# A new order of steps for three of five blocks, and scan decays by halves in two PSUM banks in one of them (state-space scan, attention and mixture-of-experts kernel)

## The reference

```python
x = x + scan_layer(group_norm(x))      # in_proj, 3x3 conv, silu, 4 scan paths, norm, gate, out_proj
t = tokens(x)
t = t + attention_causal(layer_norm(t))           # 12 heads of 16
u = layer_norm(t)
u = u + attention(ln1(u))                          # second attention, not causal
u = u + gelu(u @ mlp_w1 + b1) @ mlp_w2 + b2        # 192 -> 768 -> 192
xm = ln2(u)
u = u + sum_over_4_experts(top2_gate * (gelu(xm @ w1 + b1) @ w2 + b2))
out = t + u
```

## Time and profile before

| | us |
|---|---|
| median of 3 runs (lowest, highest) | 873.56 (868.95, 879.3) |
| the profiled execution, its own time | 875.49 |
| its span, first to last instruction | 873.8 |
| PE busy (share of the span) | 640.4 (73%) |
| DVE busy | 547.7 (63%) |
| ACT busy | 307.6 (35%) |
| POOL busy | 215.3 (25%) |
| mean granted TensorE clock | 0.846 of full speed |

### The profile page before, as it was taken

One profiled execution on the slowest core, in us unless ns is written; L12 is line 12 of the kernel. 1 busy time (PEld: TensorE's weight loads), 2 busy tenths in 40 slices (PEclk: granted clock), 3 DMA queues, 4 the chain that ended last, 5 costly groups with the idle time before them and its releaser, 6 DMA issues. The chain is left out here.

```text
span 873.8 us, 8707 instructions
## 1 busy us (share of the span) xinstructions
PE 640.4 (73%) x3156; PEld 429.7 (49%) x3156; DVE 547.7 (63%) x936; ACT 307.6 (35%) x576; POOL 215.3 (25%) x184
## 2 busy tenths in 40 slices
PE   2479556835677787858778778857787888896697
PEld 2233234423223574646346565645345657765596
DVE  4749656576998547765997556757995355442211
ACT  2324031234331132653543223563442424442131
POOL 4429511212343101031543101132452011001000
PEclk9989965757888678888899788878998899998789
DMA  6985000354670000373660003273630000000000
GB/s 143 299 170 151 0 9 1 47 145 113 161 172 25 9 1 10 48 201 93 161 152 10 9 0 38 71 191 93 175 92 9 1 1 1 1 1 10 0 1 10
DMA packets 26641, 61.69 MB, mean 71 GB/s; under 512 B 4928, under 2 KB 12752, under 8 KB 26608
## 3 DMA queue, kind: packets, MB, share of 16 engines
q1 hardware_dynamic: 26608, 61.26, 30.2%
HBM read 53.52 MB, written 3.54 MB: 65 GB/s over the span
## 5 line engine op out<-in xcount | busy, mean ns | idle before, releaser
L1895 POOL TENSOR_TENSOR state<-state,C_rows 128x1024 f32<-128x1024 f32 x42 | 113.1, 2692 | 178.4 <-DVE state L1445 156.8
L1445 DVE TENSOR_TENSOR_SCAN state<-decay,dx_rows 128x512 f32<-128x512 f32 x72 | 105.8, 1510 | 9.9 <-PE py L980 6.9
L980 PE MATMUL py<-state,sel 128*96 128x512 f32 x168 | 91.9, 681 | 14.8 <-POOL state L1895 14.6
L1765 ACT ACTIVATE decay<-d_rows,a_neg 128x255 f32<-128x255 f32 x144 | 61.1, 496 | 94.5 <-DMA d_rows<-delta_dram 58.8
L1052 PE MATMUL pd<-w_dn,act 128*128 128x192 f32 x480 | 90.5, 343 | 3.7 <-ACT act L1778 3.7
L1052 PEld LDWEIGHTS pd<-w_dn,act 128*128 128x128 f32 x480 | 82.7, 200 | 7.1 <-ACT act L1778 4.6
L1036 PE MATMUL pu<-fT,w_up 128*128 128x256 f32 x180 | 65.9, 452 | 12.4 <-ACT act L1778 11.9
L1438 DVE TENSOR_TENSOR dx_rows<-dx_rows,B_rows 128x1024 f32<-128x1024 f32 x36 | 58.4, 1621 | 12.5 <-DMA dx_rows<-delta_x_dram 12.5
L792 PE MATMUL ps<-hT,w_qkv 96*96 96x256 f32 x128 | 41.5, 495 | 33.4 <-DVE hT L1583 32.7
L1936 POOL TENSOR_TENSOR cT<-cT,inv_den 128x256 f32<-128x256 f32 x24 | 19.9, 831 | 174.3 <-DVE inv_den L1642 174.3
L1778 ACT ACTIVATE act<-pu,b_up 128x256 f32<-128x256 f32 x90 | 37.7, 470 | 71.3 <-PE pu L1040 71.1
(11 more groups left out here) (285 smaller groups left out, 1220.0 us busy)
## 6 DMA issues: line engine op xcount, KB each, us to landing
dx_rows<-delta_x_dram SPq DMA_DIRECT2D x41, 512.0 KB, 5.1
d_rows<-delta_dram SPq DMA_DIRECT2D x36, 512.0 KB, 6.6
d_rows<-delta_x_dram SPq DMA_DIRECT2D x6, 512.0 KB, 5.1
w_dn<-exp_w_dram SPq DMA_DIRECT2D x1, 2304.0 KB
B_rows<-xdbl SPq DMA_DIRECT2D x4, 512.0 KB, 7.0
C_rows<-xdbl SPq DMA_DIRECT2D x4, 512.0 KB, 10.7
w_up<-exp_w_dram SPq DMA_DIRECT2D x1, 1536.0 KB
delta_x_dram<-delta_x SPq DMA_DIRECT2D x4, 384.0 KB, 3.4
```

The source lines that it names most:

```text
L980: mm = nc.tensor.matmul(py[0:INNER, :], sel[:, first:first + INNER], flat(states[g % held])[:, paths], start=False, stop=(g == GROUPS - 1) ...
L1445: ins = nc.vector.tensor_tensor_scan(flat(states[g % held])[:, both], flat(decay[g % 2])[:, both], dx_rows[g % 2][:, both], 0.0, ALU.mult, ...
L1765: ins = nc.scalar.activation(decay[g % 2][:, k, rest], d_rows[g % 2][:, k, rest], ACT.Exp, scale=a_neg[:, at:at + 1])
L1895: nc.gpsimd.tensor_tensor(now, now, C_rows[:, :], ALU.mult).then_inc(sc_done, 1)
```

## The change

Two things change; the arithmetic does not.

1. **Plans.** `FIRST`, `STEADY` and `LAST` get new orders; `OPENING` and `CLOSING` keep theirs. Every step is still there. Steps move between slots, so only the order within each engine changes.
2. **Decays by halves.** With `one_decay = run_s and run_a and not run_f`, which holds in FIRST alone, `decays(g)` and `scan(g)` are replaced. The decays go into the PSUM banks `pu` (forward paths) and `pd` (backward paths), which no feed-forward step uses in this block. There is one such pair, not two: each half of `decays(g)` waits for the same half of scan g - 1. Instruction counts are unchanged except for two small memsets.

Of the plans, cut to what the text speaks of (before is `-`, after is `+`):

```diff
 FIRST = { "PE":
-        (0, "turned"): [("x_turn",)],
-        (0, "projected"): [("group_sums",)],
-        (0, 1): [("in_proj",)],
+        (0, "turned"): [("x_turn",), ("group_sums",)],
+        (0, 0): [("in_proj",)],
...
  "DVE":
-        (0, 2): [("silu",)],
...
-        (0, 9): [("dt", 0)],
-        (0, "spread"): [("dt", 1), ("softplus", 0), ("softplus", 1), ("softplus_log",)],
-        (0, "output"): [("scan", 0), ("scan", 1)],
+        (0, 3): [("silu",)],
...
+        (0, 11): [("dt", 0), ("dt", 1)],
+        (0, "context"): [("softplus", 0)],
+        (0, "spread"): [("softplus", 1), ("softplus_log",)],
+        (0, "output"): [("scan", 0)],
+        (1, "turned"): [("scan", 1)],
         (1, "projected"): [("scan", 2)],
         (1, 0): [("scan", 3), ("scan", 4)],
         (1, 1): [("scan", 5)],
-        (1, 3): [("scan", 6), ("scan", 7)],
-        (1, 4): [("scan", 8)],
-        (1, 5): [("scan", 9)],
-        (1, 7): [("scan", 10), ("scan", 11)],
+        (1, 3): [("scan", 6)],
+        (1, 4): [("scan", 7), ("scan", 8)],
+        (1, 5): [("scan", 9), ("scan", 10)],
+        (1, 7): [("scan", 11)],
...
  "ACT":
-        (0, "output"): [("decays", 0), ("decays", 1), ("decays", 2)],
+        (0, "output"): [("decays", 0)],
+        (1, "turned"): [("decays", 1)],
+        (1, "projected"): [("decays", 2)],
...
+        (1, 4): [("decays", 9), ("decays", 10)],
+        (1, 5): [("decays", 11)],
...
 STEADY = { "PE":
-        (0, 0): [("ffn_up", 0, 1), ("ffn_up", 0, 2)],
-        (0, 1): [("in_proj",), ("ffn_down", 0, 0), ("ffn_down", 0, 1)],
+        (0, 0): [("ffn_up", 0, 1), ("in_proj",), ("ffn_up", 0, 2)],
+        (0, 1): [("ffn_down", 0, 0)],
+        (0, 2): [("ffn_down", 0, 1)],
...
-        (1, "turned"): [("ffn_up", 3, 0)],
-        (1, "projected"): [("ffn_down", 2, 0), ("y_sum", 0), ("y_sum", 1)],
+        (1, "turned"): [("ffn_down", 1, 1), ("ffn_up", 3, 0), ("y_sum", 0)],
+        (1, "projected"): [("y_sum", 1), ("ffn_down", 2, 0)],
...
-        (1, "context"): [("y_turn",), ("ffn_down", 4, 1)],
-        (1, "spread"): [("y_out",)],
+        (1, "context"): [("y_turn",)],
+        (1, "spread"): [("ffn_down", 4, 1), ("y_out",)],
  "DVE":
-        (0, 2): [("silu",)],
-        (0, 3): [("ffn_norm", 0)],
+        (0, 2): [("ffn_norm", 0)],
+        (0, 3): [("silu",)],
...
-        (0, "output"): [("scan", 0), ("scan", 1)],
-        (1, "turned"): [("ffn_add", 1)],
+        (0, "output"): [("scan", 0)],
+        (1, "turned"): [("ffn_add", 1), ("scan", 1)],
...
-        (1, 7): [("scan", 10), ("scan", 11)],
-        (1, 8): [("ffn_add", 3)],
+        (1, 7): [("scan", 10), ("ffn_add", 3), ("scan", 11)],
  "ACT":
-        (0, 1): [("in_proj",)],
-        (0, 5): [("x_dbl", 0)],
-        (0, 7): [("x_dbl", 1), ("ffn_up", 1, 0)],
+        (0, 1): [("in_proj",), ("x_dbl", 0)],
+        (0, 3): [("x_dbl", 1)],
+        (0, 7): [("ffn_up", 1, 0)],
...
-        (1, 1): [("ffn_up", 3, 1), ("ffn_up", 3, 2), ("decays", 6)],
-        (1, 3): [("decays", 7)],
-        (1, 4): [("decays", 8)],
-        (1, 5): [("decays", 9)],
-        (1, 6): [("decays", 10), ("decays", 11)],
-        (1, 7): [("ffn_up", 4, 0)],
-        (1, 8): [("ffn_up", 4, 1)],
-        (1, 9): [("ffn_up", 4, 2)],
+        (1, 3): [("ffn_up", 3, 1)],
+        (1, 4): [("decays", 8), ("decays", 9), ("ffn_up", 3, 2), ("decays", 10)],
+        (1, 5): [("ffn_up", 4, 0)],
+        (1, 7): [("ffn_up", 4, 1), ("decays", 11)],
+        (1, 8): [("ffn_up", 4, 2)],
 LAST = { "PE":
-        (0, "projected"): [("ffn_up", 0, 0)],
-        (0, 0): [("ffn_up", 0, 1), ("ffn_up", 0, 2)],
-        (0, 1): [("ffn_down", 0, 0), ("ffn_down", 0, 1)],
-        (0, 6): [("ffn_turn", 1)],
+        (0, "turned"): [("ffn_turn", 0), ("ffn_up", 0, 0)],
+        (0, "projected"): [("ffn_up", 0, 1)],
+        (0, 0): [("ffn_up", 0, 2)],
+        (0, 1): [("ffn_down", 0, 0)],
+        (0, 3): [("ffn_down", 0, 1)],
+        (0, 8): [("ffn_turn", 1)],
...
-        (1, "projected"): [("ffn_down", 2, 0)],
-        (1, 0): [("ffn_down", 2, 1)],
-        (1, 1): [("ffn_up", 3, 1), ("ffn_up", 3, 2)],
+        (1, 0): [("ffn_down", 2, 0)],
+        (1, 1): [("ffn_up", 3, 1)],
+        (1, 3): [("ffn_up", 3, 2), ("ffn_down", 2, 1)],
```

The new functions (DVE and ACT), and SP's wait:

```diff
-                                sp.wait_ge(decay_done, g - 1)
+                                sp.wait_ge(decay_done, (g - 1) * (2 if one_decay else 1))
...
+                    def scan_by_halves(g):
+                        if g == 0:
+                            nc.vector.memset(pu[:, 0:2 * TOKENS:TOKENS], 0.0)
+                            nc.vector.memset(pd[:, TOKENS - 1:2 * TOKENS:TOKENS], 0.0).then_inc(reset_done, 1)
...
+                        for h, (bank, both) in enumerate(((pu, slice(0, 2 * TOKENS)),
+                                                          (pd, slice(4 * TOKENS - 1, 2 * TOKENS - 1, -1)))):
+                            dve.wait_ge(decay_done, 2 * g + h + 1)
+                            nc.vector.tensor_tensor_scan(
+                                flat(states[g % held])[:, both], bank[:, ::(1, -1)[h]],
+                                dx_rows[g % 2][:, both], 0.0, ALU.mult, ALU.add
+                            ).then_inc((forward_done, scan_done)[h], 1)
...
+                    def decays_by_halves(g):
...
+                        for h, (bank, used) in enumerate(((pu, forward_done), (pd, scan_done))):
+                            if g >= 1:
+                                sc.wait_ge(used, g)
+                            for k in range(2):
+                                at = g * PATHS + 2 * h + k
+                                rest = slice(1 - h, TOKENS - h)
+                                ins = nc.scalar.activation(bank[:, TOKENS * k + rest.start:TOKENS * k + rest.stop],
+                                                           d_rows[g % 2][:, 2 * h + k, rest],
+                                                           ACT.Exp, scale=a_neg[:, at:at + 1])
+                            ins.then_inc(decay_done, 1)
```

More of the change, by code:

```diff
@@ L167 @@
[L167 to L170, removed]
-        (1, "turned"): [("ffn_up", 3, 0)],
-        (1, "projected"): [("ffn_down", 2, 0), ("y_sum", 0), ("y_sum", 1)],
-        (1, 0): [("ffn_down", 2, 1), ("y_sum", 2)],
-        (1, 1): [("ffn_up", 3, 1), ("ffn_up", 3, 2), ("y_sum", 3)],
@@ L175 @@
[L175 to L181 removed]
+        (0, 0): [("ffn_up", 0, 1), ("in_proj",), ("ffn_up", 0, 2)],
+        (0, 1): [("ffn_down", 0, 0)],
+        (0, 2): [("ffn_down", 0, 1)],
+        (0, 4): [("x_dbl", 0)],
@@ new lines @@
+        (0, 5): [("x_dbl", 1)],
+        (0, 6): [("ffn_turn", 1)],
+        (0, 7): [("ffn_up", 1, 0), ("ffn_logits",)],
+        (0, 8): [("ffn_up", 1, 1), ("ffn_turn_gates",), ("ffn_bias",)],
+        (0, 9): [("dt", 0)],
+        (0, 11): [("ffn_up", 1, 2)],
+        (0, "context"): [("dt", 1)],
+        (0, "spread"): [("ffn_down", 1, 0)],
+        (0, "output"): [("ffn_up", 2, 0), ("ffn_up", 2, 1), ("ffn_up", 2, 2)],
+        (1, "turned"): [("ffn_down", 1, 1), ("ffn_up", 3, 0), ("y_sum", 0)],
@@ L192 @@
-        (0, 3): [("ffn_norm", 0)],
-        (0, 5): [("x_dbl", 0), ("ffn_norm", 1)],
-        (0, 6): [("ffn_turn", 1)],
-        (0, 7): [("x_dbl", 1)],
-        (0, 8): [("ffn_logits",)],
-        (0, 9): [("dt", 0)],
-        (0, 10): [("ffn_turn_gates",)],
-        (0, "context"): [("ffn_bias",)],
+        (0, 2): [("ffn_norm", 0)],
+        (0, 3): [("silu",)],
+        (0, 4): [("x_dbl", 0)],
+        (0, 5): [("ffn_norm", 1)],
+        (0, 7): [("ffn_turn", 1), ("x_dbl", 1), ("ffn_logits",), ("ffn_turn_gates",)],
@@ L216 @@
     "ACT": {
-        (0, "projected"): [("ffn_up", 0, 0)],
-        (0, 0): [("ffn_up", 0, 1), ("ffn_up", 0, 2)],
-        (0, 1): [("in_proj",)],
-        (0, 5): [("x_dbl", 0)],
-        (0, 7): [("x_dbl", 1), ("ffn_up", 1, 0)],
-        (0, 8): [("ffn_logits",)],
-        (0, 9): [("ffn_up", 1, 1)],
-        (0, "spread"): [("softplus", 0), ("softplus", 1), ("softplus_log",), ("ffn_up", 1, 2)],
-        (0, "output"): [("ffn_up", 2, 0), ("ffn_up", 2, 1), ("ffn_up", 2, 2), ("decays", 0), ("decays", 1),
-            ("decays", 2)],
@@ L238 @@
+        (1, 0): [("decays", 4)],
+        (1, 1): [("decays", 5)],
+        (1, 2): [("decays", 6), ("decays", 7)],
+        (1, 3): [("ffn_up", 3, 1)],
[3 more added lines that the diff above has]
+        (1, 8): [("ffn_up", 4, 2)],
     },
     "POOL": {
-        (0, "turned"): [("ffn_turn", 0)],
-        (0, "projected"): [("group_sums",)],
-        (0, 2): [("silu",)],
@@ L243 @@
[L243 to L254 removed]
+        (0, "turned"): [("ffn_turn", 0), ("group_sums",), ("ffn_norm", 0)],
@@ L255 @@
+        (0, 1): [("silu",)],
+        (0, "output"): [("times_C", 0), ("times_C", 1), ("times_C", 2), ("times_C", 3), ("times_C", 4),
+            ("times_C", 5), ("times_C", 6), ("times_C", 7)],
+        (1, 2): [("times_C", 8)],
+        (1, 6): [("ffn_norm", 1)],
+        (1, 7): [("times_C", 9), ("times_C", 10)],
```

(3 more changed lines are left out.)

193 lines of the change are left out of this document (89 added, 104 removed).

## The result

The changed kernel took 843.5 us in the median of four runs beside 876.4 for the kernel before: a ratio of 0.962, interval 0.956 to 0.968. The profiled execution took 845.55 us (span 843.8), 30.0 less than the span before. Two later comparisons gave 0.954 (0.950 to 0.958) and 0.960 (0.955 to 0.964). Ratios leave out executions over 1.5% above the fastest of their kernel, and so that of the orders alone rests on three of six and that of both fillers on two. The prediction, 846 us or 27.5 less, was right in the sum; in the profile one term had given nothing, and others more.

The account below looks back on a forecast made before the run. No engine fills a half block; the order bounds it, a chain PE, VectorE, ACT, PE, with VectorE bounding FIRST's second attention. FIRST 15, STEADY 5, LAST 7.5 sum to 27.5 off the 873.56 median: 846 us, eight in ten 829 to 863.

Parts of the forecast that it names:

- (a): FIRST's first attention: in_proj ahead of `shifted(0)` cuts VectorE's wait by 1.9 us; `silu` behind `row_max(2)` gives 0.9 more.
- (b): FIRST's first attention: `dt(1)` and `softplus(0)` move ahead of the last `invert_sums` into idle VectorE time, 2.5 us less 0.3.
- Second attention of FIRST, 10 us: FIRST's second attention: earlier `hT`, unheld scans and less idle VectorE time sum to 11.7 us, less 1.7 for possible waits.
- (c): FIRST's second attention: VectorE's copy to `hT` behind scan 0 alone comes 5.7 us earlier, 5.4 at the value copy.
- (d): FIRST's second attention: 24 scans reading decays from PSUM are not held by POOL, 34.6 to 29.0 us, 5.5 off.
- STEADY, 2.5 a turn: Each STEADY turn: new orders gain 2.5 us, 5 in all, bounds 4 against to 7 in favour a turn.
- LAST, 7.5: LAST: moved feed-forward steps shorten VectorE's waits; the end comes 7.7 us ahead, taken as 7.5, bounds 3 to 10.
- (1): Rival, PE's clock: denser PE work raises it, and with STEADY at its good end the time is 835 us; chance 0.20.
- (2): Rival, FIRST's second attention: gain becomes VectorE waits for `dx_rows` or ACT's halves, FIRST 8 us, total 853; 0.16 with (5).
- (3): Rival, STEADY and LAST: new orders only exchange stops, (c) and (d) alone remain, 864 to 870 us; chance 0.11.
- (4): Rival, ACT's queue in STEADY: gelus with table loads add 20.4 us a turn, 41 in all, 887 us; chance 0.08.
- (5): Rival, FIRST's scans: the hold came from the state buffer, so (d) is 0 and the time 852; 0.16 with (2).

Follow-up runs that it names:

- both fillers: Whole change plus matmuls whose result nobody reads, in FIRST's first attention, at LAST's end and in CLOSING, against the kernel before: ratio 0.939, median 831.7 us.

## Why the prediction was right

The sum was 27.5 and the profiled execution gained 30.0, but its terms were not met one by one: FIRST's first attention gave -0.6 for 5, its second 13.0 for 10, STEADY 8.8 for 5, LAST 8.7 for 7.5. That they came out so near together is partly luck. The three timings of the whole gave 33.5, 35 and 40 us, so the sum was low each time, mostly in FIRST, which measured 19.2 alone (15 to 23) against 15.

- **First attention of FIRST, (a) and (b), 5 us.** Right in size at a like clock (5.6 to 6.4), 0.6 us longer in the profile of the result. The step that was missing is the clock: I walked the new order with the old durations, and so with the old profile's rise at 160 us built in. Inside, in_proj's wait shrank by 1.8 for 1.9, and the hold by POOL's subtractions, a bound that I charged with nothing, cost 1.5 (VectorE's normalisation 3.68 us where the old order took 2.18).
- **Second attention of FIRST, 10 us.** Low: 13.0 in the profile. (c) is right, `hT` 5.9 us nearer the first multiplication. (d) is right to a tenth, 5.5 us of scans. The walk was off in two places that partly cancel. Groups 3 to 11 took 42.9 us (218.2 to 261.1), not 40.7, through waits of 0.70 and 0.69 us for `dx_rows` and longer multiplications. Ahead of them more was gained: counted from the first multiplication the value copy came 5.6 us earlier, as walked (5.4), and the end of scan 3 already 7.1. The first multiplication itself waited 0.8 less (2.90 beside 3.72), and one more us went behind group 11. My step "held as before" for the multiplications failed where the halves stood alone (21.0 to 19.2) and was about right in the whole (21.9).
- **STEADY, 2.5 a turn.** 3.3 in the mean of the profiles, 6.9 for both turns in the timing, against 5. The 23 loads and the wait for `decays(11)` came; six more loads cost nothing that can be seen. ScalarE had the time: 87 of 186 us busy. The drain that the Trainium skill charges with each load ("ScalarE: Activation LUTs", section "What ACT_TABLE_LOAD costs") does not show here either: 0.2 us of idle time before 11 loads, and the instruction behind a load starts 0.01 us after it in the median.
- **LAST, 7.5.** Right as a net, wrong in its parts: 9.2 in the stage less 1.7 in CLOSING, which I had called unchanged within 1 us; alone it measured 7.2. Within the stage, measured from its start, the first shift of the earlier trace rows came at 26.7 us in both profiles, not 2.1 ahead. That step of the walk was right all the same: at the clock of before it came at 24.4 us, 2.3 ahead, in three profiles of the new order, and what was missing is again the clock. In the profile of the result, the last context copy of the first attention was 3.6 ahead as said; the first shift of the second attention was 5.5 ahead, not 2.3; the end 8.7.
- **Rivals.** (1) did not come as put: the mean clock is 0.846 in both profiles. But it named the right resource. (2) holds for 1.4 us of waits. (3) is out by the runs with STEADY and LAST alone. (4) is out by the turns. (5) is out: the scans read PSUM and are not held, with the state buffer where it was.

## What to carry to other kernels

Before a stage's gain or loss is explained, compare the granted clock and the matmuls done in it in both profiles: here identical code took 69 or 78 us, and one profile alone would have told of a reorder that brings nothing. Take each stage from several executions, and read two changes apart by running each alone, for gains overlap (8.3 and 8.4 us made 14.0). Where PE is bound by its clock behind a known wait, matmuls that fill the wait without outlasting it can pay.
